# Linear attention plus fp4 FFN block on one core: the attention output projection as two fp32 products instead of three fp16 passes

## What is computed

```
xn   = layernorm(x)
qkv  = xn @ W_qkv.T            # 16 heads of 16
q    = softmax(q) / 4 ; k = exp(k)
# buckets of 64 tokens: each bucket reads the sums of k and of k*v over all earlier buckets
attn = (q @ context) / max(q . ksum, 1e-6)
a    = attn @ W_out.T          # 256 x 256: the part that the change is about
# FFN, every operand quantized to fp4 in blocks of 16 and dequantized
h    = silu(fp4(xn) @ fp4(w_gate).T) * (fp4(xn) @ fp4(w_up).T)     # 704 wide
out  = x + a + fp4(h) @ fp4(w_down).T
```

## Time and profile before

| | |
|---|---|
| median of 3 runs | 1443.69 us (1442.86 to 1446.13) |
| the profiled execution's own time | 1443.55 us |
| its span, first to last instruction | 1441.8 us |
| granted TensorE clock, mean | 0.988 of full |
| instructions | 42471 |

### The profile page before, as it was taken

One profiled execution on the slowest core, in us unless ns is written; L12 is line 12 of the kernel. 1 busy time (PEld: TensorE's weight loads), 2 busy tenths in 40 slices (PEclk: granted clock), 3 DMA queues, 4 the chain that ended last, 5 costly groups with the idle time before them and its releaser, 6 DMA issues.

```text
span 1441.8 us, 42471 instructions
## 1 busy us (share of the span) xinstructions
PE 1342.2 (93%) x10702; PEld 955.3 (66%) x10702; DVE 1342.9 (93%) x4030; ACT 1081.1 (75%) x3480; POOL 179.9 (12%) x540
## 2 busy tenths in 40 slices
PE   0149999999999999999999999999999999999997
PEld 0126777777777777777777777777777777777775
DVE  5649999999999999999999999999999999999996
ACT  1588777777777777777777777777777777777772
POOL 1521111110101010101010101010111111110100
PEclk9959999999999999999999999999999999999999
DMA  5002333233334333333333333333332333233324
GB/s 118 0 8 45 65 74 80 56 84 70 76 64 84 70 73 67 84 70 69 70 84 70 68 71 82 70 67 75 77 77 61 78 73 81 56 83 70 76 48 81
DMA packets 293240, 100.00 MB, mean 69 GB/s; under 512 B 258272, under 2 KB 292704, under 8 KB 293216
## 3 DMA queue, kind: packets, MB, share of 16 engines
q1 hardware_dynamic: 293216, 99.73, 33.0%
HBM read 19.99 MB, written 16.78 MB: 25 GB/s over the span
## 4 chain that ended last, share of the span: by engine, by line
PE 91%; ACT 3%; DVE 2%; issue 1%; ACTq 0%; DVEq 0%
PE outp L1163 11%; PE nump L1096 6%; PE unit1a L1032 5%; PE unit0a L1032 5%; PE outp L1165 5%; PE unit1a L1034 5%; PE unit1a L1036 5%; PE unit0a L1034 4%; PE unit0a L1036 4%; PE ctxp L1106 4%; PE unit1b L1034 4%; PE unit1b L1032 4%; PE unit1b L1036 4%; PE unit0b L1036 4%; PE unit0b L1032 4%; PE unit0b L1034 4%
## 5 line engine op out<-in xcount | busy, mean ns | idle before, releaser
L1163 PE MATMUL outp<-w_down_cat,q_rows 128*128 128x256 f16 x1408 | 245.7, 274 | 0.0
L593 ACT ACTIVATE snap<-ctxp,mask 64x68 f32<-64x68 f32 x1024 | 235.2, 307 | 3.2
L548 ACT ACTIVATE att_t<-trp 128x256 f16<-128x256 f32 x256 | 98.1, 383 | 111.0 <-PE trp L1118 106.5
L396 POOL TENSOR_TENSOR var_scaled<-squares,var_mul 128x1 f32<-128x1 f32 x128 | 34.4, 269 | 1134.0 <-ACT scratch L486 1126.3
L1163 PEld LDWEIGHTS outp<-w_down_cat,q_rows 128*128 128x128 f16 x1408 | 138.2, 98 | 16.3
L1165 PE MATMUL outp<-w_down_lo,q_rows 128*128 128x256 f16 x640 | 147.3, 273 | 0.0
L511 ACT ACTIVATE xnt<-trp 128x256 f16<-128x256 f32 x256 | 97.0, 379 | 58.6 <-PE trp L1058 58.6
L774 DVE TENSOR_REDUCE blk<-h 128x44 f32<-128x704 f32 x128 | 123.8, 968 | 0.1
L556 ACT ACTIVATE th<-unit1a,c_g 128x352 f32<-128x352 f32 x128 | 70.9, 554 | 58.8 <-PE unit1b L1036 58.7
L827 DVE TENSOR_TENSOR hx_v<-h,blk 128x704 f32<-128x704 f32 x128 | 111.5, 871 | 0.0
L556 ACT ACTIVATE th<-unit0a,c_g 128x352 f32<-128x352 f32 x128 | 70.8, 553 | 54.0 <-PE unit0b L1036 54.0
(11 more groups left out here) (210 smaller groups left out, 4322.5 us busy)
## 6 DMA issues: line engine op xcount, KB each, us to landing
xring<-x SPq DMA_DIRECT2D x128, 128.0 KB, 2.7
out<-xring SPq DMA_DIRECT2D x128, 128.0 KB, 2.5
xqt<-xq_s SPq DMA_TRANSPOSE x128, 2.4
q_rows<-q_rows SPq DMA_TRANSPOSE x128, 3.5
raw_qkv<-wqkv_t SPq DMA_DIRECT2D x1, 768.0 KB, 7.6
raw_gate<-wgate SPq DMA_DIRECT2D x8, 88.0 KB
raw_up<-wup SPq DMA_DIRECT2D x8, 88.0 KB
raw_down<-wdown SPq DMA_DIRECT2D x1, 704.0 KB, 6.1
```

The costliest lines, as they stand in the source:

```text
L548: nc.scalar.activation(att_t[:, par, part, :], tr32, ACT.Copy).then_inc(att_split, 1)
L593: nc.scalar.activation(kept[:, :, cols], sums[:, :, cols], ACT.Copy, scale=mask[rows, f, h:h + 1])\
L1163: nc.tensor.matmul(downp, hqt[:, par, m, :], w_down_cat[:, m, :], start=(m == 0), stop=False)
```

## The change

The attention output goes to the projection in fp32: it is transposed, copied once to SBUF as fp32, and multiplied with the unscaled fp32 weights `raw_out` in two fp32 matmuls (one for each half of the 256 inputs). `w_out` with its halves, their preparation on ACT and POOL, the subtraction `less_att` and the second ACT copy are gone. `c_o` loses the factor of w_out's scale.

```diff
-        w_out = sb("w_out", [P, 2, KC, D], fp16)
...
-        att_t = sb("att_t", [P, 2, 2, D], fp16)
+        att_t = sb("att_t", [P, 2, D])
...
-        att_less = sem("att_less")
...
# POOL
-            for n, (w, dst) in enumerate(((raw_qkv, w_qkv), (raw_out, w_out))):
+            for n, (w, dst) in enumerate(((raw_qkv, w_qkv),)):
                 pool.wait_ge(proj_hi, 2 * n + 2)
                 nc.gpsimd.tensor_tensor(dst[:, 1, :, :], w[:, :, :], dst[:, 0, :, :], ALU.subtract).then_inc(proj_lo, 1)
...
# ACT
-            def split_att(t, par, part):
-                if not is_tile(t):
-                    return
-                act.wait_ge((att_tr, att_less)[part], after(t))
-                if part == 0 and begun(t - 2):
-                    act.wait_ge(proj_done, after(t - 2))
-                nc.scalar.activation(att_t[:, par, part, :], tr32, ACT.Copy).then_inc(att_split, 1)
+            def copy_att(t, par):
+                if not is_tile(t):
+                    return
+                act.wait_ge(att_tr, after(t))
+                if begun(t - 2):
+                    act.wait_ge(proj_done, after(t - 2))
+                nc.scalar.activation(att_t[:, par, :], tr32, ACT.Copy).then_inc(att_split, 1)
...
-                split_att(k - 1, odd, 0)
+                copy_att(k - 1, odd)
                 exp_k(k + 1, odd)
-                split_att(k - 1, odd, 1)
                 exp_q(k + 1, odd)
...
-            for n, (w, dst) in enumerate(((raw_qkv, w_qkv), (raw_out, w_out))):
+            for n, (w, dst) in enumerate(((raw_qkv, w_qkv),)):
                 act.wait_ge(factors, 8)
...
# DVE
-            nc.vector.tensor_scalar(c_o[:, :], pow2[:, 0:1], pow2[:, 1:2], 2.0 ** -20, ALU.mult, ALU.mult).then_inc(factors, 1)
+            nc.vector.tensor_scalar(c_o[:, :], pow2[:, 0:1], 2.0 ** -6, None, ALU.mult).then_inc(factors, 1)
...
# PE: transpose_xn, transpose_q
-                    pe.wait_ge(att_split, after(t - 3, 2))
+                    pe.wait_ge(att_split, after(t - 3))
...
-                    pe.wait_ge(att_split, after(t - 2, 2))
+                    pe.wait_ge(att_split, after(t - 2))
...
# PE: transpose_att
-                    last = nc.tensor.matmul(tr32[:, c * P:(c + 1) * P], att[:, par, c * P:(c + 1) * P], ident32[:, :],
-                                            start=(c == 0), stop=False, is_transpose=True, skip_group_check=True)
+                    last = nc.tensor.transpose(tr32[:, c * P:(c + 1) * P], att[:, par, c * P:(c + 1) * P], ident32[:, :])
...
-            def less_att(t, par):
-                if not is_tile(t):
-                    return
-                pe.wait_ge(att_split, after(t, 2, 1))
-                nc.tensor.matmul(tr32, minus16[:, :], att_t[:, par, 0, :], start=False, stop=True, skip_group_check=True)\
-                    .then_inc(att_less, 1)
...
# PE: project_att
-                pe.wait_ge(att_split, after(t, 2))
+                pe.wait_ge(att_split, after(t))
                 if begun(t - 1):
                     pe.wait_ge(o_step, after(t - 1, 2))
                 for c in range(KC):
-                    three_passes((attp,), att_t[:, par, 0, c * P:(c + 1) * P], att_t[:, par, 1, c * P:(c + 1) * P],
-                                 (w_out[:, 0, c, :],), (w_out[:, 1, c, :],), c == 0, c == KC - 1)
+                    nc.tensor.matmul(attp, att_t[:, par, c * P:(c + 1) * P], raw_out[:, c, :], start=(c == 0), stop=(c == KC - 1))
...
-                less_att(k - 1, odd)
...
-            pe.wait_ge(proj_lo, 2)
             pe.wait_ge(prep_ev, 14)
```

## The result

| | before | after |
|---|---|---|
| median | 1444.12 us (4 runs, 1442.86 to 1446.13) | 1455.69 us (4 runs, 1455.09 to 1456.48) |
| ratio | | 1.0076, 95% interval 1.0062 to 1.009 |
| span of the profiled execution | 1441.8 | 1453.9 |
| instructions | 42471 | 41511 |

What follows compares the result with a forecast made beforehand. PE's stream was taken to bound the kernel. Per tile 0.209 + 0.05 - 0.11 = +0.149 us, +19.1 in all; with 1.2 off at start-up, 1443.55 + 19.1 - 1.2 = 1461.4 us, range 1450 to 1471 (82%).

Steps and rivals of the forecast that it cites:

- PE's stream is the pace: Steady part: PE's stream paces the kernel, so the change counts by what it does to that stream, per tile, 128 times.
- The projection, added: Attention projection on PE: two fp32 products make four records, 0.864 us a tile, +0.209 against the six fp16 products.
- The rival with one cycle a column: Projection: four fp32 records cost only 0.436 us, the tile loses 0.33, kernel ends at 1401 us, faster; chance 4%.
- Its weight loads: First fp32 load of the projection: between 0 (hidden) and +0.09 us (bare) a tile, taken as +0.05.
- The signs: Expected in the profile after: 512 records of about 380 ns, starts 0.216 apart, tile 10.54 to 10.55, DVE's wait up 0.15.
- The subtraction, removed: Context update to second gate_up matmul on PE: 0.10 to 0.12 us goes, taken as 0.11; the 0.1 hole stays.
- Start-up: w_out's preparation on ACT and POOL goes: 1.2 us off through the two ACT copies; bounds nothing and 2.9.
- DVE as the pace: Rival: DVE sets the pace and PE's 0.15 us fits beside it; 1442.3 us, no change; chance 4%.

Runs made afterwards that it cites:

- float32r: The kernel after, with the projection's two products in float32r instead of float32 and one more ACT copy at the start: 1399.5 us, ratio 0.968.
- the two start-up runs: The kernel after with POOL's w_out-sized subtraction put back (1455.97 us), and with two w_out-sized ACT copies put back (1457.57 us); one execution each.
- the last two of the timed experiments: Kernel before with one fp16 projection pass, no subtraction, one ACT copy: 1399.21 us; float32r kernel with DVE's copy of denominators moved to ACT: 1388.64 us.

## Why the prediction was right, and where it was not

- **PE's stream is the pace**: right. Both parts of the change came through at full price, alone and together (+26 and -14 make the measured 12), and the point where this ends was found, at 0.36 us a tile less.
- **The projection, added**: 0.864 forecast, 0.87 measured, from the slope of fp32 durations and the starts of paired records. The rival with one cycle a column, 0.436, is wrong for float32. A float32r record does take one cycle a column, but there a product is one record and not two, and the second waits 0.11 for its load.
- **Its weight loads**: this is the term that was mis-sized. I took +0.05 between a hidden first load and a bare one; it is hidden, 704.00 to 704.22 for the two transposes before it. I had leaned on a guess that the load would be longer than the transposes'. It is (192 ns against 142), but a load can start every 0.112 us, so its length says little of its price. 125 x 0.05 = 6.3 us, more than the 5.7 by which the forecast was too high. The Trainium skill (TensorE: Matmul & The Clock Gate, LDWEIGHTS) gives 128 / 1.2 = 107 ns for a load; the trace has 192 ns of duration, which the rule misses, and at most 112 ns of distance, which does not speak against it. The extra cost I drew from it did not come about.
- **The signs**: a tile of 10.54 to 10.55 did not come, it is 10.43. 0.05 of the difference is the load's term; the rest is that I added to the 10.40 of one tile, where the mean over all is 10.33. DVE's wait rose by 0.10 a tile, not 0.15, for the load's term again. The time was summed from the difference a tile and is free of the first slip.
- **The subtraction, removed**: 0.11 forecast. The distance from the context update to the second gate_up product fell by 0.10; adding it back cost 0.11 a tile, taking it from the kernel before gave 0.09, and 0.11 without the lower clock between 120 and 130 us. The hole at the change of shape stayed, as the first tile had shown.
- **Start-up**: 1.2 us off was near the 1.6 by which the steady part starts earlier, but by luck. The ACT copies gave nothing, POOL's piece gave 0.7 to 0.8 through L697. The rest, 0.7, was there before this part of the program: ACT's w_qkv copy already starts at 45.24 instead of 45.94, and in the two start-up runs, whose code is the same up to there, at 44.90 and 45.96, so this differs from one execution to the next and is no gain of the change. I had written that POOL's piece held nobody on the chain, though my own upper bound named the hold on DVE. What POOL's piece held was DVE's second rounding. The steady part's growth is not touched by this: 0.209 - 0.11 = 0.10 a tile.
- **DVE as the pace**: wrong for this change, as forecast. DVE's busy 10.0 of 10.33 us a tile left little, and float32r ran into it.

## What to carry to other kernels

A matmul stream is priced by distances of starts, not by counts or durations: here four fp32 records replace six fp16 ones and take a third longer, since an fp32 record holds the array two cycles a column and a product is two records. Fewer instructions and fewer copies on an engine with idle time are worth nothing by themselves; ACT's copies gave nothing here, in the tile and in the start-up. POOL's subtraction, on an engine busy 12% of the span, gave 0.7 us, because it held an instruction of DVE on the chain: what an idle engine's work delays counts, not its length. When a change goes the wrong way by a term that is known, look for another form of that term (here a single-record type), and look at once at how far the second busiest engine lets it pay. Where two engines end level, as PE and DVE do at 9.89 us here, a gain that stops says nothing of which of them stopped it.

## What the runs showed of the hardware that I had not expected

- Float32r products are one record each at one cycle a column, but two in a row start 0.22 us apart for 256 columns: the load of 190 ns starts only 0.11 us after the record before it, though fp32 loads of 192 ns start beside it and are hidden, at down to 0.112 us apart.
- DVE's small scale operation (32 columns) lasted 3.07 or 1.84 us in the start-up, ending with POOL's subtraction both times (48.34 to 51.43 in the kernel after), and POOL's 512-column subtraction lengthened a DVE operation from 2.29 to 3.01 us. POOL's own lasted 3.18 us there, longer than the 3.09 of 1536 columns, and ended at 54.23; the DVE operation that it had met ended 2.15 after that. In these pairs it looks as if each engine waited out the other's instruction. That is read from the times; no run here isolates it.
- The clock took back part of the earlier start. The stretch from 100 to 110 us has a mean granted clock of 0.72 before and 0.73 after, so with the levels 0.5 and 1 it rises at 105.6 and at 105.4 us. The kernel before issued its first context products at 105.68, at the full 2.4 GHz, and they took 0.54 us; the kernel after was there at 104.13, at 1.2 GHz, and they took 1.01. The work before was PE's first steady step after the gaps of the start-up in both. It costs 0.5 us, once, and is part of the 13.2 us above.
- The same work can meet another clock. The run without the subtraction and the one with ACT's copies put back fell to the lower level for some 3.4 us between 120 and 130 us, the kernels before and after did not, though PE did the same steps there with the same gap of 1.75 us before the context products. It explains 1.7 us each time. The seven executions of the kernel before that ran beside the last two of the timed experiments order by it too: 1442.1 us at a mean clock of 0.988, 1447.3 at 0.984. All four of the kernel after had 0.988, so at an equal clock the change costs 12 to 14 us (1442.1 to 1443.6 against 1455.7) rather than 11.6.
